# Norms finished for two steps at once, VectorE's step reordered, v copied before the transposed probabilities, one wait per matmul on TensorE

## The reference, cut to what matters

```python
for i in range(DEPTH):          # 6
    x = attn_layer(shift_tokens(x), Wqkv[i], q_scale[i], k_scale[i], Wo[i]) + x
    x = ffn_layer(shift_tokens(x), ln_g[i], ln_b[i], W1[i], b1[i], W2[i], b2[i]) + x

# in attn_layer (16 heads of 64, windows of 32 tokens that look one window back)
q, k, v = jnp.split(x @ Wqkv, 3, -1)
q = l2norm(q) * qs;  k = l2norm(k) * ksc
q = q * cos * scale + rotate_half(q) * sin * scale      # k likewise, with 1 / scale
sim = einsum('bhwie,bhwje->bhwij', q, k2) * 8.0         # masked outside the window
out = einsum('bhwij,bhwje->bhwie', softmax(sim), v2)
return out @ Wo
```

## Time and profile before

| | us |
|---|---|
| median of 3 runs (lowest to highest) | 2242.39 (2242.22 to 2244.29) |
| the profiled execution | 2249.67 |
| its span from first to last instruction | 2247.8 |
| PE busy | 2015.2 |
| DVE busy | 1627.7 |
| ACT busy | 1476.9 |
| POOL busy | 1236.7 |

### The profile page before, as it was taken

The page is one execution under the profiler, slowest core; times in us unless marked ns, Lnnn a source line. Parts: engine busy times, 40 slices in busy tenths (PEclk is TensorE's granted clock), DMA queues, the critical chain, the costliest instruction groups (busy, mean ns, idle before and its releaser), DMA issues. The chain is left out here.

```text
span 2247.8 us, 85596 instructions
## 1 busy us (share of the span) xinstructions
PE 2015.2 (90%) x32996; PEld 1382.4 (62%) x32996; DVE 1627.7 (72%) x3071; ACT 1476.9 (66%) x4549; POOL 1236.7 (55%) x1377
## 2 busy tenths in 40 slices
PE   7797988998899998899988999998999889999987
PEld 3232335875775866766757758667667577586662
DVE  1598997985875966867857759668678587596673
ACT  4522225976775966867767759668677677596772
POOL 1465865664753654754646536548546465365450
PEclk9888789999999999999999999999999999999998
DMA  1311112111121211211111211112211111121010
GB/s 57 133 66 66 65 38 78 40 40 33 42 73 30 49 38 31 66 54 37 39 33 37 78 28 50 35 36 58 62 35 41 34 37 40 28 50 30 23 29 19
DMA packets 148105, 104.49 MB, mean 46 GB/s; under 512 B 15778, under 2 KB 140256, under 8 KB 146176
## 3 DMA queue, kind: packets, MB, share of 16 engines
q1 hardware_dynamic: 147712, 99.07, 15.8%
HBM read 48.31 MB, written 1.18 MB: 22 GB/s over the span
## 5 line engine op out<-in xcount | busy, mean ns | idle before, releaser
L1372 POOL TENSOR_TENSOR QK<-PC,PS 128x256 f32<-128x256 f32 x384 | 278.5, 725 | 612.9 <-DVE PS L1283 612.9
L1121 ACT ACTIVATE PR<-ps,MN 128x64 f32<-128x64 f32 x1536 | 353.7, 312 | 378.0 <-DVE MN L1243 377.8
L1377 POOL TENSOR_TENSOR QK<-QK,RN 128x512 f32<-128x512 f32 x384 | 400.4, 1043 | 159.5 <-ACT RN L1111 132.0
L995 PE MATMUL ps<-W,XS 128*128 128x256 f32 x1536 | 401.0, 384 | 4.1 <-PEq L64 4.1
L995 PEld LDWEIGHTS ps<-W,XS 128*128 128x128 f32 x1536 | 264.7, 193 | 26.8 <-issue 4.9
L1373 POOL TENSOR_TENSOR QK<-PC,PS 128x256 f32<-128x256 f32 x384 | 278.9, 726 | 0.0
L981 PE MATMUL ps<-ident,QK 128*128 128x128 f32 x1536 | 252.7, 287 | 26.0 <-POOL QK L1377 24.1
L1267 DVE TENSOR_REDUCE SS<-SQ 128x8 f32<-128x512 f32 x384 | 259.4, 676 | 4.5 <-ACT SQ L1154 4.4
L1281 DVE TENSOR_TENSOR PC<-ps,TC 128x512 f32<-128x512 f32 x384 | 261.4, 681 | 0.3 <-issue 0.3
L1283 DVE TENSOR_TENSOR PS<-ps,TS 128x512 f32<-128x512 f32 x384 | 260.0, 677 | 0.0
L1154 ACT ACTIVATE SQ<-ps 128x512 f32<-128x512 f32 x384 | 241.4, 629 | 20.4 <-PE ps L995 11.1
(11 more groups left out here) (138 smaller groups left out, 3457.0 us busy)
## 6 DMA issues: line engine op xcount, KB each, us to landing
V<-V SPq DMA_DIRECT2D x384, 97.5 KB, 2.2
scr<-B_rows SPq DMA_DIRECT2D x32, 512.0 KB, 3.7
V<-V SPq DMA_DIRECT2D x288, 32.5 KB, 1.9
W<-in_Wqkv SPq DMA_DIRECT2D x40, 192.0 KB, 2.8
TC<-in_tcos SPq DMA_DIRECT2D x6, 1024.0 KB, 5.3
TS<-in_tsin SPq DMA_DIRECT2D x6, 1024.0 KB, 7.6
WO<-in_Wo SPq DMA_DIRECT2D x6, 512.0 KB, 5.3
W<-in_W SPq DMA_DIRECT2D x6, 341.0 KB, 3.3
```

The costliest lines, as they stand in the source:

```text
L995: mm = nc.tensor.matmul(ps[:, par, k * 2 * P:(k + 1) * 2 * P], cols[k], W[:, i, 0:2, :].rearrange("p t m -> p (t m)"), start=True, stop=True)
L1121: e = nc.scalar.activation(PR[:, m % 2, h, slot * DH:(slot + 1) * DH], ps[:, 3 + h, slot * DH:(slot + 1) * DH], ACT.Exp, scale=-1.0, bias= ...
L1372: nc.gpsimd.tensor_tensor(QK[:, par, :, 0:hd], PC[:, par, :, 0:hd], PS[:, par, :, hd:DH], ALU.add)
L1377: nc.gpsimd.tensor_tensor(QK[:, par, :, :], QK[:, par, :, :], bcast_last(RN[:, par, :], DH), ALU.mult).then_inc(qk, 1)
```

## The change

ScalarE's `logs` and `root` become one function, `norm_pair`, called first in ScalarE's step at even n only: it takes the logarithm and the exponential of 16 numbers a row, for steps n-2 and n-1 together. VectorE's `norms` now handles step n at loop count n, not n-1; it stands behind `tables`; it writes into half of a tile of 16, and takes the maximum at odd n only, by `tensor_scalar` with the constant 1e-24 in place of `tensor_tensor` with the tile LEAST. GpSimd's `rotate` moves from m = n-1 to m = n-2, with the same three instructions a step. ScalarE calls `copy_v` before `copy_p`. On TensorE each wait stands at one instruction only, mostly one wait each: the wait for `v_cp` moves from `values` to `scores`, and the wait for `pr` (PR written) from the transposes of the next step to the second half of v's projection.

```diff
@@ TensorE: scores(n)
-                wait(pe, pr, m)
-                wait(pe, oT, m - 3)
+                if n >= NSTEPS:
+                    wait(pe, pr, m)
+                    wait(pe, oT, m - 3)
                 for h in range(2):
+                    if h == 0:
+                        wait(pe, qkT, min(n - 3, NSTEPS))
+                    if h == 1 and n >= 7:
+                        pe.wait_ge(v_sh[(n - 7) % 4], 32 * ((n - 7) // 4 + 1))
                     nc.tensor.matmul(ps[:, 3 + h, 0:P], identb[:], MASKB[:, int(s == 0), h, :], ...)
-                pe.wait_ge(qkT, m + 1)
+                if n == 5:
+                    pe.wait_ge(qkT, m + 1)
+                wait(pe, v_cp, min(n, NSTEPS))
@@ TensorE: values(n)
                 pe.wait_ge(pT, m + 1)
-                pe.wait_ge(v_sh[m % 4], 32 * (m // 4 + 1))
-                wait(pe, on, m)
-                wait(pe, v_cp, min(n, NSTEPS))
+                if n >= NSTEPS + 5:
+                    pe.wait_ge(v_sh[m % 4], 32 * (m // 4 + 1))
+                    wait(pe, on, m)
@@ TensorE: project(n), the part of v
-                wait(pe, v_cp, n)
-                wait(pe, on, n - 6)
+                if n < 5:
+                    wait(pe, v_cp, n)
                 for k in range(2):
+                    if k == 0:
+                        wait(pe, on, n - 6)
+                    if k == 1:
+                        wait(pe, pr, n - 4)
...
@@ ScalarE
+            def norm_pair(n):
+                p = n // 2 - 1
+                if n % 2 or not 0 <= p < NSTEPS // 2:
+                    return
+                act.wait_ge(ssm, p + 1)
+                nc.scalar.activation(SS[:, p % 2, :], SS[:, p % 2, :], ACT.Ln, scale=LN_SCALE).then_inc(lns, 1)
+                act.wait_ge(lns, p + 1)
+                wait(act, qk, 2 * p - 2)
+                nc.scalar.activation(RN[:, p % 2, :], SS[:, p % 2, :], ACT.Exp, scale=-0.5, bias=lnb[:]).then_inc(rn, 1)
...
-                root(n)
+                norm_pair(n)
                 exponents(n)
                 copy_out(n)
                 if u == U_FFN and t >= 0:
-                    logs(n)
                     load_set(nc, act, GELU)
                 copy_qk(n)
                 squares(n)
+                copy_v(n)
                 copy_p(n)
-                copy_v(n)
                 if u == U_FFN and t >= 0:
                     gates(t, n)
                     load_set(nc, act, EXP_LN)
-                else:
-                    logs(n)
@@ VectorE
             def norms(n):
...
+                p, k = n // 2, n % 2
+                dve.wait_ge(sq, n + 1)
+                wait(dve, rn, p - 1)
+                nc.vector.tensor_reduce(SS[:, p % 2, 8 * k:8 * k + 8], SQ[:, n % 2, :, :], AX.X, ALU.add).then_inc(ss, 1)
+                if k == 1:
+                    dve.wait_ge(ss, n + 1)
+                    nc.vector.tensor_scalar(SS[:, p % 2, :], SS[:, p % 2, :], 1e-24, None, ALU.max).then_inc(ssm, 1)
...
                 least(n)
                 normalise(n)
+                tables(n)
                 norms(n)
-                tables(n)
@@ GpSimd: rotate(n)
-                m = n - 1
+                m = n - 2
...
-                pool.wait_ge(rn, m + 1)
+                pool.wait_ge(rn, m // 2 + 1)
```

More of the change, by code:

```diff
@@ L815, in transformer_block @@
         stored = [sem("stored%d" % c) for c in range(NCH)]
-        s_vz, s_ones, s_v0, s_lnb, s_least = (
-            sem(k) for k in ("s_vz", "s_ones", "s_v0", "s_lnb", "s_least"))
+        s_vz, s_ones, s_v0, s_lnb = (
+            sem(k) for k in ("s_vz", "s_ones", "s_v0", "s_lnb"))
         qkv_dram = d["Wqkv"].rearrange("l p (t i m) -> l p i t m", t=3, i=PAIRS)
@@ L925, in out_transposed @@
                     return
-                wait(pe, pr, min(n - 5, NSTEPS))
-                wait(pe, oT, m)
-                pe.wait_ge(on, m + 1)
+                if n >= NSTEPS:
+                    wait(pe, pr, min(n - 5, NSTEPS))
+                    wait(pe, oT, m)
+                    wait(pe, on, m + 1)
                 for k in range(2):
@@ L976, in qk_transposed @@
                 pe.wait_ge(qk, m + 1)
-                wait(pe, qkT, m)
+                if n < 5:
+                    wait(pe, qkT, m)
                 for x in range(2):
@@ L1007, in p_transposed @@
                     return
-                pe.wait_ge(pr, m + 1)
-                wait(pe, pT, m)
-                wait(pe, on, m)
+                if n >= NSTEPS:
+                    pe.wait_ge(pr, m + 1)
+                    wait(pe, on, m)
+                if n < 7 or n >= NSTEPS + 5:
+                    wait(pe, pT, m)
                 for h in range(2):
+                    if h == 0 and n < NSTEPS:
+                        wait(pe, oT, n - 7)
                     mm = nc.tensor.transpose(ps[:, 6, (2 + h) * P:(3 + h) * P], PR[:, m % 2, h, :], ident[:])
@@ L1174, in copy_v @@
                                ps[:, 5, 2 * P:4 * P].rearrange("p (k a d) -> p k a d", k=2, d=DH)).then_inc(v_cp, 1)
-            def logs(n):
-                m = n - 1
-                if not 0 <= m < NSTEPS:
-                    return
-                act.wait_ge(ssm, m + 1)
-                nc.scalar.activation(SS[:, m % 2, :], SS[:, m % 2, :], ACT.Ln, scale=LN_SCALE).then_inc(lns, 1)
             def deviation(t, c):
@@ L1234, in _ @@
         def _(dve):
-            dve.wait_ge(s_least, 1)
             def least(n):
@@ L1261, in norms @@
             def norms(n):
-                m = n - 1
-                if not 0 <= m < NSTEPS:
+                if n >= NSTEPS:
                     return
-                dve.wait_ge(sq, m + 1)
-                wait(dve, rn, m - 1)
-                nc.vector.tensor_reduce(SS[:, m % 2, :], SQ[:, m % 2, :, :], AX.X, ALU.add).then_inc(ss, 1)
-                dve.wait_ge(ss, m + 1)
-                nc.vector.tensor_tensor(SS[:, m % 2, :], SS[:, m % 2, :], LEAST[:], ALU.max).then_inc(ssm, 1)
+                p, k = n // 2, n % 2
[5 more added lines that the diff above has]
+                    nc.vector.tensor_scalar(SS[:, p % 2, :], SS[:, p % 2, :], 1e-24, None, ALU.max).then_inc(ssm, 1)
             def tables(n):
```

17 lines of the change are left out of this document (5 added, 12 removed).

## The result

The changed kernel takes 2291.47 us (median of 4 runs, 2287.05 to 2294.71) against 2243.34 for the one before on the same chip: ratio 1.0213, interval 1.0191 to 1.0236. It is slower, as forecast, and by more: 2273 was predicted, with 2288 as the upper end.

What follows compares the result with a forecast made beforehand. It took the plain steps as decisive, TensorE near its own pace and waiting last for V's copy. +33 (plain) + 7 - 10 + 2 - 1 = +31 on the median 2242.4 gave 2273 us; range for 8 in 10: 2246 to 2288.

Steps and rivals of the forecast that it cites:

- main term: Plain steps: V's wait ahead of `scores` closes a loop through ScalarE and VectorE, so no step is under 3.54 us.
- The handover from V's copy to the matmul: TensorE at `scores`: from V's end to the matmul 0.06 us, with 0.15 kept as the other end.
- Rival (d): Plain steps: the handover to `scores` takes 0.15 us, +22 us more, 2295 us; chance 0.07.
- The held maximum: VectorE's maximum for paired norms waits for GpSimd's second addition: 0.31 us, not 0.17; PR at 3.73; chance 0.50.
- Rival (a): VectorE's maximum runs free beside GpSimd, having one input: +13 us, 2255 us; chance 0.24.
- Rival (b): Plain steps: V's wait doesn't bind, TensorE reaches 3.23 us; 2173 us, if the loop is under 3.49; chance 0.13.
- GpSimd's index shift changes no instruction: GpSimd's `rotate`: its product comes near 4.8 us, TensorE wants it beyond 6; no cost counted.
- The feed-forward step: At u = 15 the first gate starts about 3.8 us behind PR, not 5.00: -0.95 a block, -10 us over 11.
- The steps with the mean: At u = 7 and 11 VectorE's CEN waits for reduction and maximum: 0.65 us a block, +7 us over 11.
- TensorE's waits: Bare waits cost TensorE little beside long matmuls; in plain steps the saving is hidden in 0.3 us of idle time.
- the PR wait: TensorE in v's projection: behind the output projection it costs 0 to 0.2 us a time, some 2 us in all.
- the plain steps with the tables: Plain steps: +33 us over 247; in the 20 table steps GpSimd sets the pace as before: 0, or -2.

Runs made afterwards that it cites:

- e3: Changed kernel with GpSimd's `rotate` back at m = n-1: 2263.04 us, ratio 1.0081 to the kernel before.
- e4: Changed kernel with the maximum as a `tensor_reduce` in place of `tensor_scalar`: 2257.94 us, ratio 1.0054 to the kernel before.
- e11: Changed kernel with `rotate` at n-1 and the maximum by `tensor_reduce`, V's wait still ahead of `scores`: 2241.97 us, ratio 0.9991.
- e5: Changed kernel with V's wait at `values`, `rotate` at n-1 and the maximum by `tensor_reduce`: 2205.51 us, ratio 0.9833.
- e2: Kernel before with V copied before PT and V's wait moved from `values` to `scores`: 2280.62 us, ratio 1.016.
- e6: Kernel before with only the maximum changed to a `tensor_reduce`: 2217.25 us, ratio 0.9884.
- e7: Kernel before with TensorE's waits stated once each as in the change, V's wait left at `values`: 2245.17 us, ratio 1.0003.
- e8: Kernel before with the maximum as a `tensor_reduce` and V copied before PT, V's wait still at `values`: 2202.69 us, ratio 0.9809.
- e1: Changed kernel with V's wait back at `values` (and a wait in `project` differing for the first steps): 2282.19 us, ratio 1.0167.
- e9: Changed kernel with V's wait at `values`, PT copied first and `rotate` at n-1: 2255.55 us, ratio 1.0048.

## Why the prediction was right and where it failed

**Direction and main term: right.** The loop PR, QKT, squares, V, next `scores`, MN was put at 3.54; it measures 3.53 (changed kernel, e3, e4, e11). That the wait for V is what closes it is shown from both sides: 36.5 us (e11 against e5) with the norms in pairs, 36 in the kernel before (e2), there with the longer handover in it. The handover from V's copy to the matmul was taken as 0.06: V ends at 2014.16 in the rows above, L956 starts at 2014.21, 0.05. Rival (d), which gave it 0.15, is out for this kernel; that its 2295 came nearer to the result is chance. Its price was also too high by the prediction's own terms: the long interval is set by the norms at 3.73, so a loop of 3.63 lengthens only every second step, 11 us in place of 22, thus 2284.

**The held maximum: right.** 0.31 was predicted, 0.375 is the median, and the odd interval is 3.79 against 3.73. e4 frees it and gets the predicted 3.59. Rival (a) had only the wrong instruction: a `tensor_scalar` of 16 numbers is held as the two-input one was, a reduction isn't. The Trainium skill (SBUF — State Buffer, "Who interferes with whom") makes just this division, a `tensor_scalar` may contend with GpSimd and a `tensor_reduce` never does on trn2; these runs agree, with 0.40 us against 0.19 beside the same addition. The plain steps came to 0.13 us more each, as said, though both levels lie 0.03 above the figures used: 3.53 before in place of 3.503, which was read from 22 steps of a pattern of three (3.28, 3.46, 3.80; see e6), and 3.66 after in place of 3.635. That the two errors cancel is luck. The 226 steps outside the neighbourhood of the scaled tables give +29; nearly all others of the 247 stand in the row of 40 steps, which shows -3.5. That is in part an effect of the profile of before, which has three stretches of the lower clock there; e7's profile, with one, has about 3 us less in this row.

**Rival (b): its condition was checked and not met**, since the loop was not under 3.49. e5 and e8 show what it needed: a free maximum, and V waited for at `values`.

**The failed step: "GpSimd's index shift changes no instruction", priced at 0.** The prediction followed RN and QK through a plain step, where there is indeed room (e3: plain steps 827.3 us with the shift and without). It did not ask what GpSimd's queue holds at u = 12: a wait of several us for ScalarE, which `rotate` was moved behind. Taking the shift back gives 28 us (e3): 22 in u = 13 and 14, the rest in the table steps (-3.9) and in the start (-3.5), which varies between 359 and 368 us over all these profiles and so is not the shift's. Of the 22, about 8 are the five stretches at the lower clock, 14 the late QK itself: e4 and e11 differ by the index alone, neither has a stretch there, and u = 13 and 14 take 108.1 and 94.3 us. That the drops come from the 1.5 us wait is shown only so far: they stand right behind it, and without it none is seen (e3), but six blocks here, and all eleven in e4's profile, have the same wait and no drop. The kernel before had such stretches too, at its three places among the table steps, each behind a wait of about 1.5 us for QK, so they are no property of the change alone.

**The smaller terms.** The feed-forward step: the first gate was to start 3.8 us behind PR in place of 5.00, and starts 3.99 behind it (ScalarE, changed kernel):

```profile
865.78 0.93 ACT L1139 ACTIVATE PR<-ps,MN 128x64 f32<-128x64 f32 x4 [1.11 <-DVE MN L1249]
...
869.77 1.30 ACT L1214 ACTIVATE HID<-ps,VEC 128x512 f32<-128x512 f32 x2
```

Its worth of -10 is there: in e3 the interval that ends with the squares of u = 15 takes 10.4 us less over 11 blocks. The one before it takes 3.4 more (3.58 a block in place of 3.27), which no term held, so that u = 13 and 14 together show -7 (94.2 against 101.2 us); in the changed kernel this was buried under the +22. The steps with the mean were to cost +7 and cost nothing (-0.4), though CEN does come later, 0.96 us behind the end of the squares against 0.28 before:

```profile
824.57 0.30 DVE L1276 TENSOR_SCALAR SS<-SS 128x16 f32<-128x16 f32 x1
824.78 0.68 DVE L1303 TENSOR_TENSOR CEN<-XS,ps 128x512 f32<-128x512 f32 x1
```

By steps, u = 7 takes 5.2 us more, as the late CEN would have it, and u = 6, 8 and 12 take 9.4 less; why they do was not tried out. TensorE's waits: 0 was predicted, and e7 shows 1.0003 with V waited for at `values`. With V's wait on the loop one of them may well count: the 0.09 between e2's handover and the changed kernel's is the span that the prediction had left open.

**The sum.** +31 was predicted for the profiles and +37 measured. The index shift added 22, and u = 13 another 3. The other way, the steps with the mean and the PR wait (together +9, measured -0.4) took 9 off, the plain steps with the tables 6 (32 against 26, of which the lower clock in the profile of before is a part), the start 4; filling the pipeline and the tail about cancel. So +37 lies near +31 because errors of 25 and 19 us cancel, and that is luck. The other 11 us of the 48 between the medians are the two profiled runs' places among the others, which no term could have told; the prediction laid a difference of profiles on the median without widening the range for it.

## What to carry to other kernels

When a step is moved by an index on an in-order engine, list every place where that engine waits long for something else, and look at what changes sides there: the plain steps don't show it. Put a wait for a freed buffer at the instruction that overwrites it, not ahead of work that feeds the next step's chain. And when two stalls lie in series, test them out together (e5), since either alone may only lengthen the other (e1).

## What was not expected of the hardware

A `tensor_scalar` on 16 numbers a row is held till just behind GpSimd's addition, up to 577 ns for an operation of 174; the same maximum as a reduction takes 0.19 us throughout, and in the kernel before that replacement alone is worth 1.2% (e6). Several bare waits a step between TensorE's matmuls cost nothing that can be measured (1.0003), but where the matmul waits for V's copy, 0.05 us pass if that is its only wait (changed kernel, e3, e4, e11) and 0.14 if it has another one, though that is fulfilled earlier (before, e2, e6, e7, e9). No run changes this alone. And behind one and the same wait of 1.51 us TensorE's clock fell in some blocks and not in others: TensorE was busy for 3.29 us of the 5.0 ahead of 703.5, where it fell, and for 3.26 of the 5.0 ahead of 1339, where it didn't. What decides between them stays open.

```profile
698.50:703.50 5.00, 3.29 (x82) 2.83 (x82) 4.39 (x12) 4.47 (x17) 4.49 (x6) 1.00 0.12 28
...
1334.00:1339.00 5.00, 3.26 (x83) 2.81 (x83) 4.39 (x12) 4.45 (x17) 4.52 (x6) 1.00 0.12 30
```
